# Round ends, table size and the place of the key matmul in a four-layer graph network kernel

## Chip, cores and metric

One core of one Trainium2 chip runs the whole program. The metric is the device time of one execution in microseconds (us). Engines: PE (TensorE, matmuls; PEld is its weight load), DVE (VectorE), ACT (ScalarE), POOL (GpSimd), SP (SyncE, which here only issues DMAs).

## What is computed

A graph of 3125 nodes with 32 features and 100,000 edges (src, dst, weight, 3 and 32 attributes) goes through four layers, each behind a layer norm and a ReLU and each added to x:

```
h = max(layernorm(x), 0);  x = x + L0(h)   # agg = segment_sum(edge_attr_32, src); dense 64 -> 128, batch norm, -> 32
h = max(layernorm(x), 0);  x = x + L1(h)   # radial net per edge and spherical harmonics, messages summed by dst
h = max(layernorm(x), 0);  x = x + L2(h)   # 3 times: out = clip(0.9 * A_w out + 0.1 h, 0, 1), A_w normalized weights
h = max(layernorm(x), 0);  x = x + L3(h)   # 3 times: z = batchnorm(relu(A_c z)), A_c normalized edge counts + self loop
```

A_w and A_c are 3125 by 3125 matrices, given only as edges.

## The kernel before

Nodes lie in 25 blocks of 128 (`NA`; 3200 with padding, `NP`), edges in 784 chunks of 128 (`CH`), worked through in 196 steps of four chunks (`STEPS`). The program has these stages.

**Zeroing** (0 to 213 us). POOL fills a DRAM table `both` with zeros by 40 DMAs: one pair (count, weight) of 8 bytes for each pair of nodes, 3200 by 3200 pairs.

**Phase 0** (some 50 to 1005 us), layer 0's sum over edges, while the edges are also put into the table. Four steps, k4 = 0 to 3, make one pass of a hardware loop. In each step PE multiplies a one-hot matrix with edge attributes (`scatter0`, L907, ten matmuls for two chunks, called a pair below). Beside it equal (src, dst) keys are found, so that POOL adds each key's sum once. A group is four chunks, two groups belong to a pass. `spread_keys` (L865, the **key matmul**) spreads a group's keys over the partitions into PSUM bank 7, the only one for it; ACT squares the differences (`compare_group`, L635, six operations) and makes 0/1 marks (L640); DVE keeps the earlier ones (`mark_group`, L1242); PE sums counts and weights per key (`merge_open`, L878 to L886, then `merge_hop` 1 to 3, L892, each of which waits for a flag of DVE, `live_entries`, L1290); DVE reads the result (`group_entries`, L1250 to L1255). One-hots come from ACT (L660, L665) and from DVE (L1304), the products that are multiplied from DVE (L1313). The row split of the attributes (L1301, L1309) belongs to k4 = 0. POOL's scatter-adds (L577) run beside all this, 782 in all, half of them before the feature table of layer 1 is there. Each engine runs its own list of instructions in order. On PE a step reads:

```
scatter0(s, k4, 0); scatter0(s, k4, 1)
if k4 % 2 == 0: merge_hop(g, slot, 2)
elif not is_last(s): merge_open(g, slot)
if k4 % 2 and not is_last(s, 4): spread_keys(g + 1, 1 - slot)
scatter0(s, k4, 2); scatter0(s, k4, 3)
if k4 % 2 == 0: merge_hop(g, slot, 3)
elif not is_last(s): merge_hop(g, slot, 1)
```

**Phase 1** (1060 to 2823 us), layer 1, with PE busy almost throughout.

**Rounds 0 to 2** (2825 to 3312 us), layer 2. In round 0 SP loads the table in 50 halves of a block of 128 rows (`big`, four slots); ACT takes out the weights and stores most to `adj_w` (nine blocks stay in SBUF, `kept`), DVE takes the row maxima of the counts and stores them as fp16 in `adj_c` through ACT's queue; PE multiplies (L1122). In rounds 1 and 2 the 16 streamed blocks of `adj_w` come back, and `group` (L1016) multiplies three blocks at once, on three of four column groups of 32; block 24 is a group by itself at the end. Each round ends with the sums copied out of PSUM by DVE and ACT (`copy_sums`, L1501 on DVE) and turned (L1108).

**Rounds 3 to 5** (3334 to 3481 us), layer 3 on the counts: PE multiplies three bf16 parts of z (`split_z`, in three portions of 5, 10 and 10 blocks) with the counts (L1063), first for 13 source blocks over all five banks, then the rest bank by bank; DVE reduces each bank (L1581 to L1584), takes mean and variance over the nodes (L1573 and a PE sum, L1098), and normalizes (L1597, L1598). Last, x is added (L1601), and SP stores the result.

The whole of what the change touches is printed here.

Of the kernel before, what the change touches and what calls it, by code (L numbers as in the profile page):

```python
# [25 lines left out]
P = 128  # L26
# [39 lines left out]
PER_ROUND = 2 * GROUPS + 1  # L66
# [3 lines left out]
BIG = NP * NP  # L70
CAP = 2048
SLOTS = 64
EIGHTH = NP // 8
# [4 lines left out]
EARLY = 13  # L78

# [7 lines left out]
def gnn_program(nc, x_in, src_in, dst_in, srcT_in, dstT_in, ea3_in, ea32_in, ew_in, ewT_in,  # L87
                w1T_in, b1_in, gamma_in, beta_in, w2T_in, b2_in, l1w1_in, l1b1_in, l1w2_in, l1b2_in,
                gam3_in, bet3_in, out):
    with ExitStack() as ctx:  # L90
# [296 lines left out]
        def load_half(eng, r, k, half, one):  # L387

            j = 4 * k + 2 * half + one
            m = STREAMED[2 * k + one]  # L390
            eng.dma_start(slots[:, j % 8, :],
                          adj_w[m * P:(m + 1) * P, half * HALF:(half + 1) * HALF]).then_inc(s_blk[j % 8], 16)
# [5 lines left out]
        def _(sp):  # L398
# [91 lines left out]

            pairs_of = both[0:BIG, :].rearrange("(s d) o -> s (d o)", d=NP)
# [16 lines left out]
            for r in range(1, 3):  # L508
# [19 lines left out]
            sp.wait_ge(s_out, 32)  # L528
# [3 lines left out]
        def _(pool):  # L532
# [70 lines left out]
            eighths = both[0:BIG, :].rearrange("(s d) o -> s (d o)", d=EIGHTH)  # L603
# [10 lines left out]
        def _(act):  # L614
# [125 lines left out]
            for j in range(2 * NA):  # L740
# [18 lines left out]
                if i < RING:  # L759
                    act.wait_ge(s_wcp, j + 1)  # L760
                    act.dma_start(adj_w[m * P:(m + 1) * P, half * HALF:(half + 1) * HALF],
                                  w_to).then_inc(s_wout[t], 16)
# [13 lines left out]
            def copy_sums(r):  # L776
                if r == 0:
                    act.wait_ge(s_half, NA)
                    act.wait_ge(s_full, NA)
                else:  # L780
                    act.wait_ge(s_mm, PER_ROUND * r)
# [23 lines left out]
            for r in range(1, 3):  # L805
                act.wait_ge(s_z, r + 1)

                def copy_z(g):
                    if g >= 2:
                        act.wait_ge(s_mm, PER_ROUND * (r - 1) + 2 * ((4 * g - 5) // 3 + 1))  # L810
                    n = min(4, NA - 4 * g)
# [25 lines left out]
        def _(pe):  # L837
# [86 lines left out]
            def phase0(s, k4, u):  # L924
# [7 lines left out]
                if k4 % 2 and not is_last(s, 4):  # L932
                    spread_keys(g + 1, 1 - slot)
# [66 lines left out]
            def spmm_round(r):  # L1000
                pe.wait_ge(s_z, r + 1)

                def group(k, blocks):

                    pe.wait_ge(s_zr, r * 7 + (blocks[-1] // 4 + 1))
                    for half in range(2):
                        values = []
                        for i in blocks[:-1]:
# [3 lines left out]
                        values.append(kept[:, k, half * HALF:(half + 1) * HALF])  # L1012
# [6 lines left out]
                        if k < GROUPS or half:  # L1019
                            mm.then_inc(s_mm, 1)  # L1020
# [115 lines left out]
        def _(dve):  # L1136
# [68 lines left out]
            V.scalar_tensor_tensor(out=keyT, in0=srcT, scalar=float(NP), in1=dstT, op0=ALU.mult, op1=ALU.add)  # L1205
            link(V.scalar_tensor_tensor(out=keyT_i, in0=srcT, scalar=float(NP), in1=dstT, op0=ALU.mult, op1=ALU.add))
# [5 lines left out]
            link(V.scalar_tensor_tensor(out=key[:, :], in0=src_i[:, :], scalar=float(NP), in1=dst_i[:, :],  # L1212
# [281 lines left out]
            def copy_sums(r):  # L1494
                if r == 0:
                    dve.wait_ge(s_half, NA)
                    dve.wait_ge(s_full, NA)
                else:
                    dve.wait_ge(s_mm, PER_ROUND * r)
                for n in (0, 2, 4):  # L1500
                    V.tensor_copy(aggT[:, n * 512:(n + 1) * 512], ps[:, n, :]).then_inc(s_aggc, 1)  # L1501
                dve.wait_ge(s_turn, r + 1)


            V.tensor_tensor(zn[:, :, :], h[:, :, :], over_f(dinv[:, 0, :]), ALU.mult).then_inc(s_z, 1)
# [11 lines left out]
            for r in range(3):  # L1517
                if r == 1:
                    link(V.tensor_tensor(slot_no[:, :], row_max[:, :, 0], row_max[:, :, 1], ALU.max))
                    V.tensor_scalar(flag[:, :], slot_no[:, :], float(CAP), None, ALU.is_gt).then_inc(s_flag, 1)  # L1520
# [17 lines left out]
            def split_z():  # L1538

                for a0, a1 in SPLITS:  # L1540
                    z, rest, to = zn[:, a0:a1, :], zrest[:, 0:a1 - a0, :], zparts[:, a0:a1, :, :]
# [19 lines left out]
            for e in range(8):  # L1561
# [5 lines left out]
                link(V.tensor_scalar(whole[SLOTS:P, :], whole[SLOTS:P, :], 9, None, ALU.arith_shift_right))  # L1567
                V.tensor_copy(over16[:, e * EIGHTH:(e + 1) * EIGHTH], whole).then_inc(s_over, 1)


            def over_nodes(i, r, src):

                V.tensor_reduce(fsum[:, 0, :], src.rearrange("p a f -> p f a"), AX, ALU.add).then_inc(s_fs, 1)  # L1573
# [3 lines left out]
            for r in range(3, 6):  # L1577
# [9 lines left out]
                link(V.tensor_scalar(fsum[:, 1, :], over_nodes(0, r, h[:, :, :]), 1.0 / NODES, None, ALU.mult))  # L1587
# [4 lines left out]
                V.tensor_scalar(fsum[:, 2, :], over_nodes(1, r, sq[:, :, :]), 1.0 / NODES, EPS,  # L1592
# [4 lines left out]
                link(V.tensor_tensor(sq[:, :, :], cen[:, :, :], over_a(fsum[:, 4, :]), ALU.mult))  # L1597
# [52 lines left out]
```

## Time and profile before

| what | us |
|---|---|
| median of three runs | 3483.51 |
| lowest and highest run | 3475.79, 3485.16 |
| the profiled execution, its own time | 3486.41 |
| its span in the trace | 3484.7 |

| busy in the span | us | share |
|---|---|---|
| PE | 2978.0 | 85% |
| DVE | 2742.2 | 79% |
| ACT | 2291.3 | 66% |
| POOL | 2104.3 | 60% |

The profile is one execution, taken by the hardware profiler. A timeline row gives an instruction's start, its length, engine, line, output and input; in brackets stands the idle time of the engine before it and what ended it. "issue" is time in which the engine waited for nothing that the profile shows. PEclk in a table of windows is the TensorE clock that was granted, 1.00 being 2.4 GHz. Busy shares over the whole span mix stages with different limits, so the windows of a stage say more.

### The profile page before, as it was taken

To read this page: it belongs to the slowest core of one execution; us is meant where nothing else is said; L and a number is where in the kernel's file an instruction comes from. 1 tells how busy PE (TensorE), PEld (TensorE's weight loads), DVE (VectorE), ACT (ScalarE), POOL (GpSimd) and SP (SyncE) were. 2 spreads that over 40 slices of the span, in tenths; PEclk is the share of its full clock that TensorE was granted. 3 is DMA by queue.
4 is the path that set the end of the run, shared out by engine and by line. 5 is a ranking of instruction groups with operands and counts; after the bars stand their busy time and mean duration, and the time that the engine had idled before them with its cause. 6 is when DMAs were issued, how large, how long until landed. Compare 5 with 4: busy or idle time off the path is not lost. (4 is left out here: it accounts for less than half of the span.)

```text
span 3484.7 us, 69264 instructions
## 1 busy us (share of the span) xinstructions
PE 2978.0 (85%) x19702; PEld 2385.9 (68%) x19703; DVE 2742.2 (79%) x5981; ACT 2291.3 (66%) x3192; POOL 2104.3 (60%) x1629
## 2 busy tenths in 40 slices
PE   3788788888877999999999999999999976657656
PEld 3677677777766888888888888888888841114256
DVE  6678888888877999999999999999999973450064
ACT  3678587877847888888888888888888832230000
POOL 4037888888866777777777777777777720000000
PEclk9999799899988999999999999999999987798878
DMA  9953222222213333333333333333333369999830
GB/s 402 422 188 36 12 15 16 14 15 15 15 6 67 52 50 52 52 52 50 52 52 51 52 52 52 50 52 52 51 51 52 52 242 426 425 389 377 362 139 6
DMA packets 265841, 397.89 MB, mean 114 GB/s; under 512 B 149901, under 2 KB 200836, under 8 KB 259252
## 3 DMA queue, kind: packets, MB, share of 16 engines
q0 software_dynamic: 149184, 124.54, 21.1%
q1 hardware_dynamic: 100180, 199.71, 16.9%
q10 hardware_dynamic: 16416, 72.92, 5.1%
q8 instruction: 28, 0.46, 0.1%
q14 instruction: 33, 0.27, 0.0%
HBM read 264.96 MB, written 132.05 MB: 114 GB/s over the span
## 5 line engine op out<-in xcount | busy, mean ns | idle before, releaser
L577 POOL DMA_INDIRECT both<-kept x782 | 1295.9, 1657 | 443.4 <-issue 205.1
L916 PEld LDWEIGHTS ps<-prod,big 128*128 128x128 f32 x7840 | 1134.3, 190 | 136.8 <-DVE prod L1283 133.2
L916 PE MATMUL ps<-prod,big 128*128 128x170 f32 x7840 | 1183.2, 310 | 22.2 <-DVE prod L1283 16.7
L585 POOL DMA_INDIRECT kept<-feat_dram,kept x782 | 760.8, 973 | 279.8 <-issue 232.2
L907 PE MATMUL ps<-prod,onehot 128*128 128x320 f32 x3920 | 719.4, 339 | 133.5 <-ACT onehot L665 116.2
L660 ACT ACTIVATE big<-iota_b,kept 128x640 f32<-128x640 f32 x1029 | 779.0, 815 | 13.6
L907 PEld LDWEIGHTS ps<-prod,onehot 128*128 128x128 f32 x3920 | 639.6, 207 | 167.9 <-issue 121.1
L665 ACT ACTIVATE big<-big 128x2560 f32<-128x2560 f32 x196 | 458.1, 2337 | 275.3 <-PE ps L916 275.2
L981 PE MATMUL ps<-w2mix,kept 65*128 65x384 f32 x1568 | 559.3, 500 | 21.6 <-ACT kept L712 21.6
L1455 DVE TENSOR_REDUCE kept<-kept 128x80 f32<-128x1280 f32 x392 | 562.0, 1474 | 0.0
L981 PEld LDWEIGHTS ps<-w2mix,kept 65*128 65x128 f32 x1568 | 284.1, 191 | 179.7 <-issue 23.5
L1445 DVE TENSOR_TENSOR kept<-ps,kept 128x384 f32<-128x384 f32 x784 | 396.3, 546 | 0.0
L608 POOL DMA_INDIRECT prod<-both,row_idx x8 | 7.8, 978 | 539.8 <-DVE row_idx L1560 525.8
L635 ACT ACTIVATE kept<-ps,kept 128x128 f32<-128x128 f32 (+2 forms) x588 | 225.0, 482 | 151.2 <-PE ps L865 151.2
L1313 DVE TENSOR_TENSOR prod<-kept 128x1280 fp32r<-128x1280 f32 x196 | 292.3, 1491 | 1.9
L1122 PE MATMUL ps<-big,zring 128*32 128x512 f32 (+3 forms) x400 | 184.8, 619 | 121.6 <-DMA big<-both 110.2
L1304 DVE TENSOR_SCALAR onehot<-iota_b,kept 128x640 fp32r<-128x640 f32 x539 | 285.7, 583 | 0.1
L1441 DVE TENSOR_TENSOR kept<-ps,kept 128x512 f32<-128x512 f32 x392 | 266.9, 681 | 0.0
L1122 PEld LDWEIGHTS ps<-big,zring 128*32 128x32 f32 x400 | 45.4, 125 | 261.0 <-issue 249.2
L1513 DVE TENSOR_REDUCE row_max<-big 128x1 f32<-128x1600 f32 x50 | 91.0, 1819 | 163.7 <-DMA adj_c<-kept 110.4
L757 ACT ACTIVATE kept<-big 128x1600 f32<-128x1600 f32 x50 | 82.2, 1648 | 192.3 <-issue 76.3
L1283 DVE TENSOR_TENSOR prod<-high,kept 128x680 f32<-128x680 f32 (+1 forms) x196 | 170.3, 869 | 43.8 <-DVE kept L1464 43.4
(232 smaller groups left out, 2988.8 us busy)
## 6 DMA issues: line engine op xcount, KB each, us to landing
both<-big POOLq DMA_DIRECT2D x40, 2000.0 KB, 96.2
big<-both SPq DMA_DIRECT2D x50, 1600.0 KB, 10.7
adj_w<-kept ACTq DMA_DIRECT2D x32, 800.0 KB, 33.3
big<-adj_w SPq DMA_DIRECT2D x32, 800.0 KB, 12.1
big<-adj_w ACTq DMA_DIRECT2D x32, 800.0 KB, 11.7
kept<-keys_dram SPq DMA_DIRECT2D x196, 128.0 KB, 3.0
kept<-in_wT SPq DMA_DIRECT2D x196, 128.0 KB, 3.0
adj_c<-kept ACTq DMA_DIRECT2D x42, 400.0 KB, 32.5
```

What stands on the lines that cost most here:

```text
L577: pool.indirect_dma_start(both, bass.IndirectOffsetOnAxis(ap=sc_idx[:, c:c + 1], axis=0), sc_val[:, c // 2, c % 2, :], None, compute_op=AL ...
L585: pool.indirect_dma_start(gath[:, s % 2, k, :], None, feat_dram, bass.IndirectOffsetOnAxis(ap=src_i[:, 4 * s + k:4 * s + k + 1], axis=0)). ...
L660: act.activation(dist[:, k, :], iota_b[:, :], ACT.Square, scale=-1.0, bias=bcol[:, ds(4 * s + k, 1)]).then_inc(s_dist[n], 4 // len(ks))
L665: act.activation(to[:, q, 0:len(ks), :], dist[:, 0:len(ks), :], ACT.Relu, scale=-1.0, bias=1.0).then_inc(s_oh[n], 1)
L907: mm = pe.matmul(ps[:, SUM0[part], 0:HI * 2 * FEAT], onehot0[:, q, k, part * P:(part + 1) * P], prod0[:, q, k, :, :].rearrange("p a m -> p ...
L916: mm = pe.matmul(part_sums(part, MSG), onehot[:, q, k, part * P:(part + 1) * P], prod[:, q, k, 0:HI * MSG], start=False, stop=False, skip_ ...
L981: mm = pe.matmul(ps[:, 4 + k, 0:384], hidT[:, q, k * P:(k + 1) * P], w2mix[:, :], start=True, stop=True)
L1304: ins = V.tensor_scalar(onehot0[:, q, k, :], iota_b[:, :], b_src[:, ds(4 * s + k, 1)], None, ALU.is_equal)
L1313: V.tensor_tensor(prod0[:, q, :, :, :], high0[:, ds(4 * s, 4), :].unsqueeze(3) .broadcast_to([P, 4, HI, 2 * FEAT]), rows0[:, 4 * k4:4 * k4 ...
L1441: V.tensor_tensor(T[:, :, 0:256].rearrange("p k (o x) -> p k o x", o=16), ps[:, 4 + 2 * g:6 + 2 * g, 0:256].rearrange("p k (o x) -> p k o ...
L1445: ins = V.tensor_tensor(T[:, k, 256:640].rearrange("p (u i x) -> p u i x", u=8, i=3), ps[:, 4 + 2 * g + k, 256:384].rearrange("p (u x) -> ...
L1455: V.tensor_reduce(res[:, q, 2 * g:2 * g + 2, 0:40], terms[:, g, :, :].rearrange("p k (o x) -> p k o x", x=16), AX, ALU.add).then_inc(s_red, 1)
```

## The change

1. *Key matmul.* `spread_keys` for the group after next is called in the even steps, behind `merge_hop` 2, instead of in the odd steps behind `merge_open`.
2. *Table.* `both` has 3126 rows (nodes and one for padding edges) of 3128 pairs. Zeroing, keys, loads and stores of round 0, loads of rounds 1 and 2 and the rows read for round 3 follow: second halves are 1528 columns wide instead of 1600, and block 24 is loaded with 54 rows.
3. *Last block in the last group.* Block 24 joins the eighth group, which now has four blocks.
4. *Sums copied by halves.* The banks that the first half of the last group completes are copied as soon as that half is done.
5. *Mean by bank.* In rounds 3 to 5 DVE sums each bank over its nodes when the bank is reduced.
6. *Normalization and result in portions.* The last two operations of a round go portion by portion, ahead of `split_z` for that portion; the result is normalized, added and stored in two portions.

The core of the diff, in which DVE's new function is called where the whole-width operations stood:

```diff
-PER_ROUND = 2 * GROUPS + 1
+PER_ROUND = 2 * GROUPS
-BIG = NP * NP
+TROWS = NODES + 1
+TCOLS = -(-TROWS // 8) * 8
+TABLE = TROWS * TCOLS
+BIG = -(-TABLE // (ZERO_PIECES * 2 * P)) * (ZERO_PIECES * 2 * P)
+WIDE = (HALF, TCOLS - HALF)
-EIGHTH = NP // 8
+EIGHTH = TCOLS // 8
+OUTS = ((0, 13), (13, NA))
...
-                sp.dma_start(big[:, j % 4, :],
-                             pairs_of[m * P:(m + 1) * P, half * NP:(half + 1) * NP]).then_inc(s_ld[j % 4], 16)
+                rows = min(P, TROWS - m * P)
+                sp.dma_start(big[0:rows, j % 4, 0:2 * WIDE[half]],
+                             pairs_of[m * P:m * P + rows, half * NP:half * NP + 2 * WIDE[half]]).then_inc(s_ld[j % 4], 16)
...
-            sp.wait_ge(s_fin, 1)
-            sp.dma_start(out[0:(NA - 1) * P, :].rearrange("(a b) f -> b a f", b=P),
-                         x[:, 0:NA - 1, :]).then_inc(s_out, 16)
+            for i, (a0, a1) in enumerate(OUTS):
+                sp.wait_ge(s_fin, i + 1)
+                whole = min(a1, NA - 1)
+                sp.dma_start(out[a0 * P:whole * P, :].rearrange("(a b) f -> b a f", b=P),
+                             x[:, a0:whole, :]).then_inc(s_out, 16)
...
                 for n in (1, 3, 5, 6):
                     c0, w = NCOL[n]
+                    if r == 0:
+                        act.wait_ge(s_half if n == 1 else s_full, NA)
+                    else:
+                        act.wait_ge(s_mm, PER_ROUND * r - (n == 1))
                     act.activation(aggT[:, c0:c0 + w], ps[:, n, 0:w], ACT.Copy).then_inc(s_agga, 1)
...
-                if k4 % 2 and not is_last(s, 4):
-                    spread_keys(g + 1, 1 - slot)
+                if k4 % 2 == 0 and not is_last(s, 4):
+                    spread_keys(g + 2, slot)
...
-                for k in range(GROUPS):
+                for k in range(GROUPS - 1):
                     group(k, (3 * k, 3 * k + 1, 3 * k + 2))
-                group(GROUPS, (NA - 1,))
+                group(GROUPS - 1, (NA - 4, NA - 3, NA - 2, NA - 1))
...
                 for n in (0, 2, 4):
+                    if r == 0:
+                        dve.wait_ge(s_full if n == 4 else s_half, NA)
+                    else:
+                        dve.wait_ge(s_mm, PER_ROUND * r - (n < 4))
                     V.tensor_copy(aggT[:, n * 512:(n + 1) * 512], ps[:, n, :]).then_inc(s_aggc, 1)
...
+            def normal(r, a0, a1):
+
+                n = a1 - a0
+                link(V.tensor_tensor(h[:, a0:a1, :], cen[:, a0:a1, :],
+                                     fsum[:, 4, :].unsqueeze(1).broadcast_to([P, n, FEAT]), ALU.mult))
+                link(V.tensor_tensor(h[:, a0:a1, :], h[:, a0:a1, :],
+                                     bet3[:, r - 3, :].unsqueeze(1).broadcast_to([P, n, FEAT]), ALU.add))
...
+                    link(V.tensor_reduce(fsum[:, 5 if b else 0, :], h[:, mine, :].rearrange("p a f -> p f a"), AX,
+                                         ALU.add))
+                    if b:
+                        ins = V.tensor_tensor(fsum[:, 0, :], fsum[:, 0, :], fsum[:, 5, :], ALU.add)
...
-                link(V.tensor_tensor(sq[:, :, :], cen[:, :, :], over_a(fsum[:, 4, :]), ALU.mult))
-                link(V.tensor_tensor(h[:, :, :], sq[:, :, :], over_a(bet3[:, r - 3, :]), ALU.add))
                 if r < 5:
-                    split_z()
-            V.tensor_tensor(x[:, :, :], x[:, :, :], h[:, :, :], ALU.add).then_inc(s_fin, 1)
+                    split_z(r)
+            for a0, a1 in OUTS:
+                normal(5, a0, a1)
+                V.tensor_tensor(x[:, a0:a1, :], x[:, a0:a1, :], h[:, a0:a1, :], ALU.add).then_inc(s_fin, 1)
```

How the order of instructions changes at three places. (ISA and REGISTER_ALU rows are waits and address arithmetic; lines of the change are numbered in its own file: L872 is the key matmul, L899 a hop, L914 the pair, L1024 `group`, L1115 the turn.)

PE, phase 0, in the loop before, an odd step from the end of `merge_open` to the first pair of the next even step and its hop 2:

```order
L886 MATMUL ps<-kept 128x1
L862 ISA
L864 REGISTER_ALU
L865 MATMUL ps<-kept,places 128x512
L907 MATMUL ps<-prod_49,onehot_50 128x320 x10
L892 MATMUL ps<-kept 128x1
L902 REGISTER_ALU
L905 ISA
L907 MATMUL ps<-prod_49,onehot_50 128x320 x10
L892 MATMUL ps<-kept 128x1
```

And in the changed kernel, an even step from its first pair to hop 3:

```order
L914 MATMUL ps<-prod_49,onehot_50 128x320 x10
L898 ISA
L899 MATMUL ps<-kept 128x1
L869 ISA
L871 REGISTER_ALU
L872 MATMUL ps<-kept,places 128x512
L914 MATMUL ps<-prod_49,onehot_50 128x320 x10
L898 REGISTER_ALU
L899 MATMUL ps<-kept 128x1
```

The key matmul stood behind the last matmul of `merge_open` (L886), ahead of the odd step's second pair; it now stands between hop 2 and hop 3, ahead of the even step's second pair.

PE, end of round 1 before, the second half of the eighth group (`big` holds two streamed blocks, `kept` the third), then block 24 alone, then the turn:

```order
L1016 MATMUL ps<-big,zring 32x512 x2
L1016 MATMUL ps<-kept,zring 32x512
L1016 MATMUL ps<-big,zring 32x128 x2
L1016 MATMUL ps<-kept,zring 32x128
L1016 MATMUL ps<-kept,zring 32x512 x3
L1016 MATMUL ps<-kept,zring 32x64
L1016 MATMUL ps<-kept,zring 32x448
L1016 MATMUL ps<-kept,zring 32x512 x2
L1016 MATMUL ps<-kept,zring 32x128
L1108 MATMUL ps<-stack_id,prod 128x32 x25
```

And in the changed kernel:

```order
L1024 MATMUL ps<-big,zring 32x512 x2
L1024 MATMUL ps<-kept,zring 32x512 x2
L1024 MATMUL ps<-big,zring 32x128 x2
L1024 MATMUL ps<-kept,zring 32x128 x2
L1115 MATMUL ps<-stack_id,prod 128x32 x25
```

The eight matmuls of the lone block are gone from behind the group; each piece of the group has two of `kept` instead of one.

DVE, end of round 5 before, from the variance on:

```order
L1592 TENSOR_SCALAR fsum<-ps 128x32
L1595 RECIPROCAL fsum<-fsum 128x32
L1596 TENSOR_TENSOR fsum<-fsum,gam 128x32
L1597 TENSOR_TENSOR both_tmp<-both_tmp,fsum 128x800
L1598 TENSOR_TENSOR h<-both_tmp,bet 128x800
L1601 TENSOR_TENSOR x<-x,h 128x800
```

And in the changed kernel:

```order
L1620 TENSOR_SCALAR fsum<-ps 128x32
L1623 RECIPROCAL fsum<-fsum 128x32
L1624 TENSOR_TENSOR fsum<-fsum,gam 128x32
L1586 TENSOR_TENSOR h<-both_tmp,fsum 128x416
L1588 TENSOR_TENSOR h<-h,bet 128x416
L1629 TENSOR_TENSOR x<-x,h 128x416
L1586 TENSOR_TENSOR h<-both_tmp,fsum 128x384
L1588 TENSOR_TENSOR h<-h,bet 128x384
L1629 TENSOR_TENSOR x<-x,h 128x384
```

The three operations of full width became two portions of three, and the first portion's result is there before the second is begun.

## Rows read from the trace of the kernel before

**Rows 1.** Windows: length, busy PE, PEld, DVE, ACT, POOL, PEclk, DMA share, GB/s.
```profile
100.00:200.00 100.00, 78.95 (x562) 69.44 (x561) 70.86 (x161) 70.57 (x111) 0.00 (x0) 0.95 1.02 422
220.00:1005.00 785.00, 661.39 (x4652) 590.43 (x4651) 649.60 (x1371) 605.46 (x934) 646.21 (x385) 0.90 0.26 17
2900.00:3050.00 150.00, 93.29 (x182) 22.34 (x183) 59.74 (x45) 35.27 (x24) 0.00 (x0) 0.76 1.01 426
```

**Rows 2.** Waits, 600 to 1000 us: waiting line, releaser, us in total, times, longest.
```profile
ACT kept L635 <- PE ps L865: 56.2, 42, 2.3
PE ps L907 <- ACT onehot L665: 54.1, 33, 2.1
```

**Rows 3.** Timeline of ACT, phase 0, first comparison of a set of four steps.
```profile
681.45 2.30 ACT L635 ACTIVATE kept<-ps,kept 128x128 f32<-128x128 f32 x6 [0.97 <-PE ps L865]
...
701.45 2.30 ACT L635 ACTIVATE kept<-ps,kept 128x128 f32<-128x128 f32 x6 [2.30 <-PE ps L865]
...
718.95 2.30 ACT L635 ACTIVATE kept<-ps,kept 128x128 f32<-128x128 f32 x6 [0.98 <-PE ps L865]
...
981.33 2.29 ACT L635 ACTIVATE kept<-ps,kept 128x128 f32<-128x128 f32 x6 [2.31 <-PE ps L865]
```

**Rows 4.** Windows, the stretch behind 690 us, columns as in rows 1.
```profile
690.00:695.00 5.00, 5.00 (x30) 4.35 (x29) 3.07 (x6) 3.67 (x7) 4.39 (x3) 0.50 0.33 28
```

**Rows 5.** Timeline of PE, phase 0.
```profile
688.20 1.85 PE L907 MATMUL ps<-prod,onehot 128*128 128x320 f32 x10 [2.09 <-ACT onehot L665]
...
708.20 1.73 PE L907 MATMUL ps<-prod,onehot 128*128 128x320 f32 x10 [2.07 <-ACT onehot L665]
...
710.18 0.38 PE L865 MATMUL ps<-kept,places 3*128 3x512 bf16 x1
710.50 1.73 PE L907 MATMUL ps<-prod,onehot 128*128 128x320 f32 x10
...
712.11 1.73 PE L907 MATMUL ps<-prod,onehot 128*128 128x320 f32 x10
```

**Rows 6.** Timeline of DVE, phase 0.
```profile
706.18 0.16 DVE L1290 TENSOR_SCALAR kept<-ps 128x1 bf16<-128x1 f32 x1
...
710.42 1.49 DVE L1313 TENSOR_TENSOR prod<-kept 128x1280 fp32r<-128x1280 f32 x1
...
715.50 0.16 DVE L1290 TENSOR_SCALAR kept<-ps 128x1 bf16<-128x1 f32 x1
...
718.60 1.49 DVE L1313 TENSOR_TENSOR prod<-kept 128x1280 fp32r<-128x1280 f32 x1
```

**Rows 7.** Timeline of POOL, the first add and the first load of the feature table.
```profile
222.06 1.90 POOL L577 DMA_INDIRECT both<-kept  x1 [181.14 <-DMA both<-big]
...
1058.52 1.02 POOL L585 DMA_INDIRECT kept<-feat_dram,kept  x1 [35.10 <-DMA feat_dram<-big]
```

**Rows 8.** Timeline of DVE, end of round 0.
```profile
3137.32 1.89 DVE L1501 COPY prod<-ps 128x512 f32<-128x512 f32 x3 [3.15 <-issue]
```

**Rows 9.** Chain of waits, end of round 1: start, us, what.
```profile
3196.70 12.61 DMA big<-adj_w
...
3209.44 2.89 PE ps L1016 x26
...
3212.41 4.26 PE ps L1016 x13
...
3216.69 0.70 DVE prod L1501
```

**Rows 10.** Chain of waits, end of round 4 and start of round 5.
```profile
3424.25 0.34 DVE h L1583
...
3424.97 1.50 DVE fsum L1573
...
3433.86 1.00 DVE h L1598
...
3436.99 15.75 PE ps L1063 x325
```

More of the change, by code:

```diff
@@ L390, in load_half @@
             m = STREAMED[2 * k + one]
-            eng.dma_start(slots[:, j % 8, :],
-                          adj_w[m * P:(m + 1) * P, half * HALF:(half + 1) * HALF]).then_inc(s_blk[j % 8], 16)
+            eng.dma_start(slots[:, j % 8, 0:WIDE[half]],
+                          adj_w[m * P:(m + 1) * P, half * HALF:half * HALF + WIDE[half]]).then_inc(s_blk[j % 8], 16)
         block = ctx.enter_context(nc.Block())
@@ L760, in _ @@
                     act.wait_ge(s_wcp, j + 1)
-                    act.dma_start(adj_w[m * P:(m + 1) * P, half * HALF:(half + 1) * HALF],
-                                  w_to).then_inc(s_wout[t], 16)
+                    act.dma_start(adj_w[m * P:(m + 1) * P, half * HALF:half * HALF + WIDE[half]],
+                                  w_to[:, 0:WIDE[half]]).then_inc(s_wout[t], 16)
                 act.wait_ge(s_ccp, j + 1)
@@ L1007, in group @@
                         values = []
-                        for i in blocks[:-1]:
+                        for i in blocks[:2]:
                             j = 4 * k + 2 * half + len(values)
@@ L1011, in group @@
                             values.append(slots[:, j % 8, :])
-                        values.append(kept[:, k, half * HALF:(half + 1) * HALF])
+                        for i in blocks[len(values):]:
+                            values.append(kept[:, k + i - blocks[2], half * HALF:(half + 1) * HALF])
                         for c0, w, bank, col in pieces[half]:
@@ L1204, in _ @@
             dve.wait_ge(s_in["idxT"], 32)
-            V.scalar_tensor_tensor(out=keyT, in0=srcT, scalar=float(NP), in1=dstT, op0=ALU.mult, op1=ALU.add)
-            link(V.scalar_tensor_tensor(out=keyT_i, in0=srcT, scalar=float(NP), in1=dstT, op0=ALU.mult, op1=ALU.add))
+            V.scalar_tensor_tensor(out=keyT, in0=srcT, scalar=float(TCOLS), in1=dstT, op0=ALU.mult, op1=ALU.add)
+            link(V.scalar_tensor_tensor(out=keyT_i, in0=srcT, scalar=float(TCOLS), in1=dstT, op0=ALU.mult, op1=ALU.add))
             V.tensor_scalar(digit_i[:, 0, :], keyT_i, 16, None, ALU.arith_shift_right)
@@ L1211, in _ @@
             dve.wait_ge(s_in["idx"], 32)
-            link(V.scalar_tensor_tensor(out=key[:, :], in0=src_i[:, :], scalar=float(NP), in1=dst_i[:, :],
+            link(V.scalar_tensor_tensor(out=key[:, :], in0=src_i[:, :], scalar=float(TCOLS), in1=dst_i[:, :],
                                         op0=ALU.mult, op1=ALU.add))
@@ L1519, in _ @@
                     link(V.tensor_tensor(slot_no[:, :], row_max[:, :, 0], row_max[:, :, 1], ALU.max))
-                    V.tensor_scalar(flag[:, :], slot_no[:, :], float(CAP), None, ALU.is_gt).then_inc(s_flag, 1)
+                    V.scalar_tensor_tensor(out=flag[:, :], in0=slot_no[:, :], scalar=float(CAP), in1=valid[:, :],
+                                           op0=ALU.is_gt, op1=ALU.mult).then_inc(s_flag, 1)
                 copy_sums(r)
@@ L1536, in _, with split_z @@
             layernorm()
-            def split_z():
+            def split_z(r=None):
                 for a0, a1 in SPLITS:
+                    if r is not None:
+                        normal(r, a0, a1)
                     z, rest, to = zn[:, a0:a1, :], zrest[:, 0:a1 - a0, :], zparts[:, a0:a1, :, :]
@@ L1591, in _ @@
                 link(V.tensor_tensor(sq[:, :, :], cen[:, :, :], cen[:, :, :], ALU.mult))
[L1592 removed]
+                V.tensor_reduce(fsum[:, 0, :], sq[:, :, :].rearrange("p a f -> p f a"), AX, ALU.add).then_inc(s_fs, 1)
+                V.tensor_scalar(fsum[:, 2, :], over_nodes(1, r), 1.0 / NODES, EPS,
                                 ALU.mult, ALU.add).then_inc(s_var, 1)
@@ L1625, in chunks @@
         return a.reshape((CH, P) + a.shape[1:]).swapaxes(0, 1).reshape(P, -1)
-    src, dst = (chunks(k, NP - 1) for k in ("src", "dst"))
+    src, dst = (chunks(k, NODES) for k in ("src", "dst"))
     w = chunks("edge_weight", 0)
```

35 lines of the change are left out of this document (15 added, 20 removed).

## The prediction, made before the change was timed

> **What bounds the kernel now.** I read the windows first, to split the 3484.7 us into stretches with different limits, then waits and timelines inside those that the change touches. The profiled execution took 3486.4 us, 2.9 above the median of the three runs (3483.5), so I sum against 3486.4 and take 2.9 off at the end. A difference of 0.3% (10.5 us) is about what a measurement of this kernel can tell from none. Zeroing the table and round 0 run at the rate of the DMA engines, 422 and 426 GB/s at a share of 1.0 [rows 1]; there bytes are time. Phase 0 (220 to 1005 us) is held by no single engine: no busy time fills its 785 us [rows 1], so a loop of waits sets it. Phase 1 is not touched.
>
> In phase 0 the reader should see one loop. ACT's group comparison waits for the key matmul, 42 times and 56 us in 400; PE waits for ACT's one-hots, 33 times and 54 us [rows 2]. From 701.45 to 718.95 four steps take 17.50 us; from 681.45 to 701.45 they take 20.00; from 701.45 to 981.33, 15 sets of four, the mean is 18.66 [rows 3]. In the 20.00 PE's clock is at 1.2 instead of 2.4 GHz for a stretch, 0.50 granted with PE full [rows 4]. Just before, PE had stood still for 2.09 us waiting for ACT (688.20). An equal pause, 2.07 us at 708.20 [rows 5], lies in the 17.50 set. So the plain loop is 17.50, a fall of the clock costs about 2.5, and (18.66 - 17.50) / 2.5 = 0.46 falls come per set. 785 / 18.66 gives 42 sets; I count 41, leaving one out for work that the stretch holds once.
>
> **The key matmul.** It moves from the odd step, behind merge_open, into the even step before, behind hop 2. Same count; what changes is what stands ahead of it. ACT's path (key matmul 710.18 [rows 5], compare, one-hots, pair on PE, merge_open, key matmul) opens: the keys are there one to two pairs earlier. Left is the loop between DVE and PE. On DVE hop 3 is seen at 715.50, then come group entries, marks and one-hots up to the product at 718.60, 3.10 us, and the product, 1.49 [rows 6]. On PE, pair and hop take 712.11 - 710.50 = 1.61 and the key matmul 710.50 - 710.18 = 0.32 [rows 5], so two pairs with hops and the key matmul, which this loop now carries, are 3.54. That is 8.1 us for a half; the half with the row split starts at 706.18 and reaches its product at 710.42: 4.24 + 1.49 + 3.54 = 9.3. Their sum is 17.4, plus four handovers between engines of some 0.1: 17.8. I take 17.7; the bounds are 17.4, with no handover, and 18.1, with handovers of nearly 0.2. The loop itself thus gains nothing: +0.2 a set. Nor should the matmul wait for its row bank, since ACT's first six squares (2.30 us from their start [rows 3]) come before that point.
>
> What moves is PE's pause. The single wait of two microseconds for ACT goes; waits for the product of some 1.3 remain. If half the falls go, a set loses 0.58 instead of 1.16: 17.7 + 0.58 = 18.28, -0.38 by 41 = **-15**. Bounds: all falls gone, -40, and POOL, which waits 35.1 us for the feature table [rows 7], allows some 44 with its earlier start; one fall in every set, 17.7 + 2.5 = 20.2, **+63**. I take the middle because half of the long pauses here were followed by no fall. The loads of key parts on SP's queue are released by the key matmul of two groups before, so they move with it and keep a lead of a whole set, and the attribute loads queued behind them come no later: nothing. If that lead were short, the next key matmul would be late, which is case D.
>
> **The table.** 3126 rows of 3128 pairs instead of 3200 by 3200: 78.2 MB instead of 81.9, 3.7 MB at 422 GB/s = 8.8 us less zeroing. It lets POOL start at 213 instead of 222.06, and this is hidden behind POOL's 35.1 us [rows 7]. Phase 0 beside it wins the little that it runs faster without the DMA load, **-1** (0 to -2). In round 0 each of 24 second halves loads 576 bytes a row less (1.77 MB), the last block 54 rows instead of 128 (1.92 MB), and the stores of weights are narrower (0.59 MB): 4.28 MB / 426 = 10.0 us. The end of that stretch isn't bound by bytes: the copies start at 3137.32, after 3.15 in which DVE waits for a last store, past all loads [rows 8]; that tail stays. I take **-8** between -10 and -3. The low end is for stores that end little earlier than now, and for the row pitch of 25,024 bytes, which is no multiple of 256: the nearest rows with different streams, 422 and 426, differ by 1%, 2 us on the 78 MB read here.
>
> The Trainium skill has two rules against this part, which no run here shows yet. "DMA: Bandwidth & Descriptors", how a descriptor splits into AXI transactions: one that starts off a 256-byte boundary fetches from the boundary below. Estimated from that page, some 3 beats on 400 a row, 1.4 us for the whole read. The same page, why a DMA increments its semaphore by 16: the engines used are the largest number up to 16 that divides the rows, so 54 rows would go by 9; the last 1.35 MB would take 5.6 us instead of 3.2, and my -8 would be about -4.
>
> **The ends of rounds 1 and 2.** The lone last block costs 4.26 us on the chain behind the last three-block half of 2.89 [rows 9]. Now it rides as a fourth column group with the other three, on rows of the array that they leave free. If a half with four costs what one with three does, all 4.26 goes; if it adds by matmuls, 2.89 by 4/3 is 0.96 more and -3.3 is left. Copying the first half's sums while the second runs hides the 0.70 of DVE at 3216.69 [rows 9]. Narrower loads, 0.59 MB a round, give 1 where DMA bounds the round (12.61 us of load in the chain). I take **-6** for round 1 and **-5** for round 2, whose end is bound by PE; bounds -13 and -7 together. In round 0 the split copies gain nothing, since that last store precedes them.
>
> **The count rounds.** A mean by bank: rounds 4 and 5 have DVE waiting between banks, so only the last bank's reduce (0.34, as the operation of that width at 3424.25) and a small add, some 0.2 by estimate, stand in place of 1.50 [rows 10]: -0.9 each. In round 3, where DVE runs the banks back to back, five reduces and four adds replace it: +1.0. The normalization in portions: the first fifth needs two operations of 0.34 instead of two of 1.00 [rows 10], -1.3 in rounds 3 and 4. PE's early pass takes 15.75 us for 13 source blocks [rows 10], so 6 for the first five; the second portion's eight operations of some 0.5 lie under it, uncovered they would cost 1. Result in two portions: two more small operations, half the output earlier, -0.2. Together +1.0 - 1.8 - 2.6 - 0.2 = -3.6, **-4** (-5 to 0).
>
> **Sum.** -15 - 1 - 8 - 6 - 5 - 4 = -39; 3486.4 - 39 = 3447.4, less 2.9: 3444.5, **3445**.
>
> **The rivals.**
> (A) *The clock stays up.* With the long pause gone, no falls: -40 instead of -15, 3420. For it: such a pause stands ahead of the fall at 690. Against it: the pause at 708.20 did nothing.
> (B) *Falls in every set, the slower case.* The pauses before the products recur in each half, evenly, and the clock falls once a set: +63 in place of -15, 3445 + 78 = 3523. It decides from a loss of (39 - 15) / 41 = 0.59 us a set over today's: then the other gains are used up, 3484. For it: today's sets already show 0.46 falls without anything that prevents more. Against it: PE's pauses become shorter.
> (C) *Falls as before, and a loop as long as I take it or longer.* 17.7 to 18.1 plus 1.16: +0.2 to +0.6 by 41 = +8 to +25, the rest -24: 3468 to 3485. For it: DVE is busy 650 of 785 us [rows 1], and the key matmul now stands in its loop; PE does the same work in sets of about the old length. The Trainium skill ("TensorE: Matmul & The Clock Gate", part 1) has the clock set "based on how busy the PE has been recently"; by that rule moved pauses alone change nothing, and this case holds. The trace so far bears it out in one thing, that an equal pause is followed by a fall only at times.
> (D) *The move doesn't open ACT's loop*, since the matmul must wait for ACT's squares from the group before (one row bank): phase 0 as now, 3460.
>
> **How the numbers follow.** My forecast 0.40, A 0.23, B 0.08, C 0.22, D 0.07. Faster by more than 0.3% (under 3473): forecast, A, D and 0.08 of C, 0.78. Within: 0.13 of C. Slower: B and the last of C, 0.09. The range from 3413 (A with the best of the other bounds) to 3484 (C) leaves B and some margin out.
>
> **What would show it.** ACT's wait for the key matmul nearly gone and PE's for ACT's one-hots with it, PE's weight loads waiting for DVE's product instead; compares every 17.4 to 18.1 us where the clock holds; granted clock over phase 0 above 0.90 (A: near 1; B: 0.83 or less). POOL's first add near 213 and its wait for the feature table longer than 35, or shorter if phase 0 shrinks by more. Round 0's last copy 8 us earlier relative to its start, the lone group of 4.26 absent. I am wrong if phase 0 lasts as long as before with a steady clock, if the load of 54 rows is slow, or if the four-block half takes 7 us.

## The result, and the profile after

The changed kernel takes 3462.99 us (median of 7 runs, 3448.94 to 3469.85) against 3482.31 for the kernel before: a ratio of 0.994, 95% interval 0.9929 to 0.9952. It is faster, by 19 us; 38 were forecast. (Each ratio here is to the kernel before, timed beside the kernel in question.) The profiled execution has a span of 3465.3 us, 19.4 below that of before, so the stages can be compared directly. Each line of the table runs from one event in the two traces to the next:

| stage, from one event to the next | before | after | difference | forecast |
|---|---|---|---|---|
| start to POOL's first gather from the feature table | 1058.5 | 1057.6 | -0.9 | -16 |
| to DVE's first reduction of round 0 | 1776.4 | 1774.9 | -1.5 | 0 |
| to the copies of round 0's sums | 302.4 | 298.8 | -3.6 | -8 |
| to the end of round 1's turn | 86.6 | 81.6 | -5.0 | -6 |
| to the end of round 2's turn | 98.3 | 92.8 | -5.5 | -5 |
| to the end (rounds 3 to 5, result) | 162.5 | 159.7 | -2.8 | -4 |

The events in the changed kernel are POOL's first gather (1057.58) and DVE's first reduction (2832.51) in the rows below, the copies at 3131.27, and the DVE operation behind each turn (the chain's rows L1531). Of before, the three that stand in no group of rows are these, from the timeline of DVE and from the chain of waits:

```profile
2834.95 1.82 DVE L1513 TENSOR_REDUCE row_max<-big 128x1 f32<-128x1600 f32 x1
```

```profile
3223.92 1.07 DVE both_tmp L1523 x2
...
3322.18 1.07 DVE both_tmp L1523 x2
```

Most of what is missing, 15 of 20 us, is missing ahead of phase 1. There the changed kernel's rows look as if the change had worked. Windows, as [rows 1]:

```profile
220.00:1005.00 785.00, 675.75 (x4749) 582.40 (x4749) 670.73 (x1421) 604.17 (x948) 654.38 (x365) 0.98 0.25 17
```

Waits from 600 to 950 us, as [rows 2]:

```profile
ACT onehot L673 <- PE ps L914: 48.9, 20, 2.7
PEld ps L914 <- DVE prod L1320: 35.5, 39, 1.5
PE ps L914 <- DVE prod L1320: 32.2, 39, 1.4
```

Timeline of ACT, first comparison of a set, as [rows 3]:

```profile
432.27 2.28 ACT L643 ACTIVATE kept<-ps,kept 128x128 f32<-128x128 f32 x6
...
699.78 2.28 ACT L643 ACTIVATE kept<-ps,kept 128x128 f32<-128x128 f32 x6
...
717.45 2.28 ACT L643 ACTIVATE kept<-ps,kept 128x128 f32<-128x128 f32 x6
...
931.54 2.28 ACT L643 ACTIVATE kept<-ps,kept 128x128 f32<-128x128 f32 x6
```

The granted clock is 0.98 where it was 0.90. ACT's wait for the key matmul has left the list, PE and its weight loads wait for DVE's product, and ACT waits for PE instead. A set of four steps takes 17.67 us (699.78 to 717.45), and 17.83 as the mean of 28 sets (432.27 to 931.54), where the mean was 18.66. So phase 0 did get shorter, by 28.6 us up to the point where SP stores the finished feature table (timeline of SP, before and changed):

```profile
1051.95 0.38 SPq L454 DMA_DIRECT2D feat_dram<-big  x1
```

```profile
1023.34 0.38 SPq L459 DMA_DIRECT2D feat_dram<-big  x1
```

But POOL's timeline, as [rows 7], takes it back:

```profile
211.90 1.68 POOL L585 DMA_INDIRECT both<-kept  x1 [170.98 <-DMA both<-big]
...
1055.73 1.54 POOL L585 DMA_INDIRECT both<-kept  x1 [0.30 <-issue]
1057.58 1.02 POOL L593 DMA_INDIRECT kept<-feat_dram,kept  x1 [0.30 <-issue]
```

The adds begin 10 us earlier and end 34 us later. The 35 us in which POOL waited for the feature table are gone, not because the table is late but because POOL is. 392 adds take 1057.3 - 211.9 = 845 us, 2.16 each; before it was (1023.4 - 222.1) / 392 = 2.04.

### The profile page after: what moved, and what is told of

Same layout as the page of the kernel before. It is cut to its first block and busy times, and to the rows that moved or that the text cites. A ratio compares the mean times of both kernels' runs of the same rounds, so it can differ in the third digit from the quotient of the medians.

```text
span 3465.3 us, 69301 instructions
## 1 busy us (share of the span) xinstructions
PE 2974.6 (86%) x19703; PEld 2370.4 (68%) x19703; DVE 2742.9 (79%) x6018; ACT 2280.7 (66%) x3192; POOL 2141.3 (62%) x1629
## 3 DMA queue, kind: packets, MB, share of 16 engines
q1 hardware_dynamic: 100034, 195.42, 16.6%
## 5 line engine op out<-in xcount | busy, mean ns | idle before, releaser
L585 POOL DMA_INDIRECT both<-kept x782 | 1333.0, 1705 | 439.8 <-issue 194.6
L923 PE MATMUL ps<-prod,big 128*128 128x170 f32 x7840 | 1183.2, 310 | 22.5 <-DVE prod L1290 17.4
L668 ACT ACTIVATE big<-iota_b,kept 128x640 f32<-128x640 f32 x1029 | 779.0, 815 | 13.6
L914 PE MATMUL ps<-prod,onehot 128*128 128x320 f32 x3920 | 684.5, 325 | 81.2 <-DVE prod L1320 79.6
L914 PEld LDWEIGHTS ps<-prod,onehot 128*128 128x128 f32 x3920 | 597.7, 194 | 112.9 <-DVE prod L1320 84.5
L1311 DVE TENSOR_SCALAR onehot<-iota_b,kept 128x640 fp32r<-128x640 f32 x539 | 291.4, 593 | 0.0
L673 ACT ACTIVATE onehot<-big 128x640 fp32r<-128x640 f32 x196 | 171.1, 873 | 182.4 <-PE ps L914 173.7
```

The source lines that it names most:

```text
L585: pool.indirect_dma_start(both, bass.IndirectOffsetOnAxis(ap=sc_idx[:, c:c + 1], axis=0), sc_val[:, c // 2, c % 2, :], None, compute_op=AL ...
L668: act.activation(dist[:, k, :], iota_b[:, :], ACT.Square, scale=-1.0, bias=bcol[:, ds(4 * s + k, 1)]).then_inc(s_dist[n], 4 // len(ks))
L673: act.activation(to[:, q, 0:len(ks), :], dist[:, 0:len(ks), :], ACT.Relu, scale=-1.0, bias=1.0).then_inc(s_oh[n], 1)
L914: mm = pe.matmul(ps[:, SUM0[part], 0:HI * 2 * FEAT], onehot0[:, q, k, part * P:(part + 1) * P], prod0[:, q, k, :, :].rearrange("p a m -> p ...
L923: mm = pe.matmul(part_sums(part, MSG), onehot[:, q, k, part * P:(part + 1) * P], prod[:, q, k, 0:HI * MSG], start=False, stop=False, skip_ ...
L1311: ins = V.tensor_scalar(onehot0[:, q, k, :], iota_b[:, :], b_src[:, ds(4 * s + k, 1)], None, ALU.is_equal)
```

## Experiments

The theory, P: POOL's adds are the path from the end of the zeroing to phase 1, and the moved matmul makes each of them slower. The rivals: the table's new row pitch slows them (Q), or the moved matmul brought its share and something else took it (R).

### The key matmul alone, and all but the key matmul

The first is the kernel before with

```diff
-                if k4 % 2 and not is_last(s, 4):
-                    spread_keys(g + 1, 1 - slot)
+                if k4 % 2 == 0 and not is_last(s, 4):
+                    spread_keys(g + 2, slot)
```

> The kernel before with the key matmul moved and nothing else. Theory P (POOL's scatter-adds took over as the bound): phase 0 on PE, DVE and ACT ends some 40 us earlier, with the granted clock near 0.98 over it, but the 392 adds start at 222 us as before and take 2.16 us each instead of 2.04, so they end at about 1068; POOL no longer waits for the feature table, and the kernel is about 9 us slower than before, 3491 us. Rival Q (the new table's row pitch slows the adds, not the moved matmul): adds at 2.04, ending at 1023, and the kernel is 35 us faster, 3447.

The second is the changed kernel with these lines as they were before.

> The changed kernel with the key matmul put back. P: the clock falls again, phase 0 ends near 1004, the adds take 2.04 us each and end near 1013, POOL waits some 40 us for the feature table, phase 1 starts near 1057 as in the changed kernel: the same time within 4 us, 3463. Rival Q: adds at 2.16 with the old place of the matmul too. Rival R (the moved matmul did bring its 15 us, and something else took them): 3478.

Measured: the matmul alone makes the kernel slower, 3496.31 us, ratio 1.0035 (1.0017 to 1.0053). Everything but the matmul gives 3464.36 us, ratio 0.9948 (0.9931 to 0.9966), the changed kernel's time. POOL's timeline with the matmul alone, then with all but it:

```profile
220.64 1.90 POOL L577 DMA_INDIRECT both<-kept  x1 [179.73 <-DVE kept L1255]
...
1064.35 1.02 POOL L585 DMA_INDIRECT kept<-feat_dram,kept  x1 [0.30 <-issue]
```

```profile
1055.41 1.02 POOL L593 DMA_INDIRECT kept<-feat_dram,kept  x1 [40.66 <-DMA feat_dram<-big]
```

The adds' groups from 430 to 940 us (count, busy time, mean ns), in this order: before, changed, matmul alone, all but the matmul:

```profile
L577 POOL DMA_INDIRECT both<-kept x253 | 421.8, 1667 | 88.3 <-issue 88.3
```

```profile
L585 POOL DMA_INDIRECT both<-kept x238 | 427.3, 1796 | 84.5 <-issue 78.6 <-DMA both<-kept 4.2 <-DVE kept L1262 1.7
```

```profile
L577 POOL DMA_INDIRECT both<-kept x238 | 428.8, 1802 | 82.0 <-issue 78.5 <-DMA both<-kept 3.5
```

```profile
L585 POOL DMA_INDIRECT both<-kept x254 | 420.3, 1655 | 90.2 <-issue 86.8 <-DMA both<-kept 3.4
```

An add takes 1.80 us wherever the matmul has moved and 1.66 wherever it hasn't, with either table. Q falls, R too. What the moved matmul gives on PE it costs on POOL, and with the new table it hardly matters whether POOL or the feature table is last: 1057.6 against 1055.4.

### Why an add becomes slower

Two adds from the changed kernel's timelines beside DVE's products:

```profile
608.13 1.49 DVE L1320 TENSOR_TENSOR prod<-kept 128x1280 fp32r<-128x1280 f32 x1
...
612.78 1.48 DVE L1320 TENSOR_TENSOR prod<-kept 128x1280 fp32r<-128x1280 f32 x1
```

```profile
608.38 2.65 POOL L585 DMA_INDIRECT both<-kept  x1 [0.30 <-issue]
611.34 1.54 POOL L585 DMA_INDIRECT both<-kept  x1 [0.30 <-issue]
613.34 2.33 POOL L585 DMA_INDIRECT both<-kept  x1 [0.46 <-issue]
```

Both long adds start inside a product and end 1.41 us behind its end (608.38 + 2.65 against 608.13 + 1.49; 613.34 + 2.33 against 612.78 + 1.48); the one between takes its plain 1.54. From 430 to 940 us, 48 of the 238 adds start inside a product and are lengthened by it, to 2.33 us each, and end 1.41 to 1.44 us behind the product's end. In the kernel before it is 37 of 253, 2.10 us each, with the same distance. Adds that start in the last 0.13 us of a product aren't lengthened, which fits: 1.54 - 0.13 = 1.41. The product holds the add up until it ends, and in the changed kernel more adds meet one, and nearer to its start.

The product isn't the only operation that does it. The row split's two operations do too, L1308 (one SBUF input) and L1316 (two), as these rows of DVE and of POOL show, with ends 1.41 and 1.42 us apart:

```profile
601.77 0.42 DVE L1308 TENSOR_SCALAR kept<-kept 128x512 int32<-128x512 int32 x1
...
603.81 0.67 DVE L1316 TENSOR_TENSOR kept<-kept 128x512 f32<-128x512 f32 x1
```

```profile
601.82 1.78 POOL L585 DMA_INDIRECT both<-kept  x1 [0.30 <-issue]
603.91 1.99 POOL L585 DMA_INDIRECT both<-kept  x1 [0.30 <-issue]
```

DVE's one-hots (L1311) do it as well. All the adds' time over 1.54 us from 430 to 940 us is 60.8 us in the changed kernel (0.26 an add) and 32.1 before (0.13). The products make 37.9 of it, the row split 15.0, the one-hots 7.7; before it was 20.6, 1.6 and 9.7. So the products are some 60% of what an add lost, and the row split, which hardly any add met before, is the rest.

The Trainium skill ("SBUF — State Buffer", SBUF: two separate sides) has VectorE and GpSimd share one pair of ports, as an exclusive lock: an operation of VectorE in a 2-port mode, or one with two SBUF inputs against a GpSimd operation that reads SBUF, takes it for the whole instruction if it starts first. The holds by the products and by L1316 agree with that; whether L1308 and L1311 run in a 2-port mode no run shows. By the same rule a GpSimd operation that starts first keeps the other out for its whole length, and in that the trace doesn't agree: 92 of the changed kernel's 114 products start while an add is under way for more than 0.06 us, and none of these takes more than 1.50 us.

If the product holds the adds, shorter products must hold them for less:

```diff
-                V.tensor_tensor(prod0[:, q, :, :, :], high0[:, ds(4 * s, 4), :].unsqueeze(3)
+                for o in (0, 2):
+                    V.tensor_tensor(prod0[:, q, o:o + 2, :, :], high0[:, ds(4 * s + o, 2), :].unsqueeze(3)
...
```

> The changed kernel with DVE's product of a step of phase 0 in two halves of 0.75 us. If an add that meets a product waits for that one instruction to end, the halves cut the delay: adds at some 2.05 us, POOL done near 1016, 3463 - 40 = 3423. If adds lose by DVE's total time, or by something else: adds at 2.16 as before, 3463, or a little more for the added DVE instructions.

Measured: 3446.96 us, ratio 0.9894 (0.9878 to 0.9911), 16 us under the changed kernel. The adds' group again, and the first gather:

```profile
L585 POOL DMA_INDIRECT both<-kept x250 | 423.9, 1696 | 89.0 <-issue 85.1 <-DVE kept L1262 2.3 <-DMA both<-kept 1.6
```

```profile
1039.96 1.02 POOL L593 DMA_INDIRECT kept<-feat_dram,kept  x1 [16.56 <-DMA feat_dram<-big]
```

The adds end at 1023.4, 2.07 us each, near the 2.05 that the theory had; from 430 to 940 us the products hold them for 16.8 us instead of 37.9, though DVE's work is longer. Only now the feature table is last, at 1040, so the gain is 16 and not 40. (The longer DVE work makes a set 18.0 us.)

### What POOL's queue is worth, and phase 1's pace

Leave 24 adds out, and nothing else: `for c in range(CH // 2 - 24): add(c)`, with the later counts of landed adds lowered by 12 for each parity.

> The changed kernel without the last 24 of the 392 adds that go ahead of layer 1 (chunks 368 to 391 never reach the table, so the time is that of 24 adds fewer). P: 24 x 2.16 = 52 us less on POOL, the feature table at about 1018 is then last, phase 1 starts there: 3463 - 39 = 3424. If phase 1's start isn't held by POOL's adds: 3463.

Measured: 3442.29 us, ratio 0.9884 (0.9867 to 0.9902): 21 us, where 39 were expected.

```profile
1028.08 1.02 POOL L595 DMA_INDIRECT kept<-feat_dram,kept  x1 [22.78 <-DMA feat_dram<-big]
```

Phase 1 starts 29.5 us earlier, behind the feature table, which I had put at 1018 and which lands at 1028. The profiled spans, of one execution each, differ by 26.9 us, the medians by 21. So 29.5 us is what the changed kernel loses to POOL's adds at the start of phase 1. Can the adds simply go later?

```diff
-            for c in range(CH // 2):
+            for c in range(CH // 2 - 24):
                 add(c)
...
+                    late = max(0, 24 - (s - BEHIND + 1) // 8)
+                    upto = min(2 * (STEPS + s - BEHIND) + 2 - late, USED)
+                    for c in range(added[0], upto):
+                        add(c)
```

> The changed kernel with 24 of the 392 adds ahead of layer 1 moved into phase 1, one more in every eighth step. Theory P2 (POOL also sets phase 1's pace, its queue never waits there by more than 0.3 us): phase 1 starts at 1028 as in drop24, but takes 24 x 1.9 = 46 us more: 3463 - 29 + 46 = 3480. Rival (PE sets phase 1's pace and POOL has slack): 3442 as in drop24.

> As shift24, but the 24 adds come in twos, one pair more in every sixteenth step, so that an even add never follows the odd one it waits for within a step more often than in the changed kernel; in shift24 the odd shift put such a wait of up to 3.5 us in half the steps. P2 (POOL sets phase 1's pace): start at 1028, phase 1 longer by 24 x 1.9 = 46 us: 3480. Rival (POOL has slack in phase 1): 3442 as in drop24.

Measured: 3735.93 us, ratio 1.0722 (1.0699 to 1.0745), and in pairs 3522.81 us, ratio 1.0111 (1.0093 to 1.0129). The first was a badly made experiment. In the second half of the edges an even add waits until the odd one before it has landed; the shift by one put the two side by side, as in this row of its timeline, in step after step:

```profile
1804.39 1.58 POOL L586 DMA_INDIRECT both<-kept  x1 [2.20 <-issue]
```

In pairs this is left to about a dozen steps. First gather and first reduction of round 0 there:

```profile
1033.70 1.02 POOL L594 DMA_INDIRECT kept<-feat_dram,kept  x1 [24.57 <-DMA feat_dram<-big]
```

```profile
2890.89 1.82 DVE L1525 TENSOR_REDUCE row_max<-big 128x1 f32<-128x1600 f32 x1
```

That is 1857 us instead of 1775: 82 more, 46 of them for 24 adds of 1.9 us, most of the rest in thirteen such waits of 2.1 to 3.1 us, 34 in all. There is no slack to shift into; POOL sets phase 1's pace too. PE's busy share there, 98% (1731.6 of the 1763 us from 1060 to 2823 in the changed kernel), hid it: POOL's own waits from 1100 to 2800 are of 0.3 us at most.

### The table alone

The changed kernel with `TROWS = NP` (and the two operations that clear the columns beyond the table left out, since there are none):

> The changed kernel with the table at 3200 by 3200 pairs again. Theory P (POOL is the bound from the end of the zeroing to the end of phase 1): POOL starts its adds 9 to 10 us later and all of it arrives, phase 1 starts at 1067; with round 0 longer by 4 and the other rounds by 1 or 2, 3463 + 15 = 3478 us. By the recorded prediction the zeroing is hidden and round 0 is worth 8: 3463 + 10 = 3473, with phase 1 starting at 1058.

Measured: 3485.91 us, ratio 1.0011 (0.9995 to 1.0026).

```profile
220.48 1.68 POOL L585 DMA_INDIRECT both<-kept  x1 [179.57 <-DMA both<-big]
...
1071.17 1.02 POOL L593 DMA_INDIRECT kept<-feat_dram,kept  x1 [0.30 <-issue]
```

Without the smaller table nothing is left of the gain: phase 1 starts 12.7 us later than in the kernel before, and the 13.4 us that the last four parts of the change give in rounds 1 to 5 only make up for it. Against the changed kernel, POOL starts 8.6 us later and gathers 13.6 later (its adds take 2.17 instead of 2.16); round 0 takes 303.7 instead of 298.8. The table is worth 18.6 us in the profiled spans and 23 in the medians, of which I had booked 9, and the zeroing's part of it at nothing.

### The last block's load

> The changed kernel with each load of block 24 (54 rows) cut into 48 and 6 rows. Theory (a load of 54 rows goes by few DMA engines: the last loads ran at 111 to 209 GB/s where the kernel before had 418 to 438): the last loads come back to over 300 GB/s and the time from DVE's first reduction of round 0 to its copies of the sums falls from 298.8 us by 2 to 5. Rival (the end waits for stores of counts): 298.8 as it is.

The edit: `for r0, r1 in ((0, 48), (48, 54))`, two loads for each half of block 24. One execution, 3466.17 us. Timeline of DVE, first reduction, the first wait of the tail, the copies; first of the changed kernel, then with the loads cut:

```profile
2832.51 1.82 DVE L1520 TENSOR_REDUCE row_max<-big 128x1 f32<-128x1600 f32 x1
...
3103.60 1.82 DVE L1520 TENSOR_REDUCE row_max<-big 128x1 f32<-128x1600 f32 x1 [9.40 <-DMA adj_c<-prod]
...
3115.73 1.82 DVE L1520 TENSOR_REDUCE row_max<-big 128x1 f32<-128x1600 f32 x1 [4.70 <-DMA adj_c<-prod]
...
3131.27 1.89 DVE L1507 COPY prod<-ps 128x512 f32<-128x512 f32 x3 [3.17 <-issue]
```

```profile
2832.20 1.82 DVE L1522 TENSOR_REDUCE row_max<-big 128x1 f32<-128x1600 f32 x1
...
3104.12 1.82 DVE L1522 TENSOR_REDUCE row_max<-big 128x1 f32<-128x1600 f32 x1 [9.69 <-DMA adj_c<-prod]
...
3131.48 1.89 DVE L1509 COPY prod<-ps 128x512 f32<-128x512 f32 x3 [3.15 <-issue]
```

299.3 us against 298.8: nothing. Nor did the last loads' rate come back (238, 151 and 133 GB/s in the 5 us from 3110, 3115 and 3120). The tail waits for stores of counts to free their staging, 9.4, 2.0, 4.7 and 1.7 us ahead of four of its last six reductions, and 9.7, 2.0, 4.4, 1.0 and 0.7 with the loads cut. So the rule of the Trainium skill ("DMA: Bandwidth & Descriptors", why a DMA increments its semaphore by 16) by which 54 rows go by 9 engines is neither shown nor refuted here; the 2.4 us estimated from it don't show in the stage's time.

### Looking for a faster kernel

Three more cuts of the product, each with PE waiting for less than the whole: in the first `scatter0` waits for `4 * s + (2 if k < 2 else 4)` of the halves' increments, in the second only in odd steps, in the third there are four quarters and it waits for `4 * s + k + 1`.

> As split_prod, and PE's first two scatters of a step wait for the first half of the product alone. In split_prod POOL's adds ended at 1023 and the feature table at 1040 was last (3447 us), so there PE, DVE and ACT's loop was the bound again. Theory: the loop between DVE and PE loses most of one half-product, 0.7 us, per pair of steps, the feature table is ready before 1020, and POOL is last again at 1025 to 1045, since denser products slow its adds: 3432 to 3450 us. Rival: the loop is not that of DVE and PE, and the first half buys nothing: 3447.

Measured: 3453.58 us, ratio 0.9907 (0.9885 to 0.9929). A set falls to 16.6 us (29 sets from 429.2 to 911.1), so it was the loop between DVE and PE that set a set's length. The last copy into the feature table starts at 974.1, but POOL arrives at 1045.0, 2.12 us an add: more than 60 us of slack for PE, DVE and ACT, and a slower kernel than with plain halves.

```profile
974.10 0.42 DVE L1427 COPY big<-h 128x400 f32<-128x400 f32 x1
```

```profile
1045.00 1.03 POOL L593 DMA_INDIRECT kept<-feat_dram,kept  x1 [0.30 <-issue]
```

> As split_prod, with PE's first two scatters waiting for the first half of the product in the odd steps alone. In split_prod the feature table was last, 17 us behind POOL's adds, in split_prod2 POOL was last, at 2.12 us an add. Theory P: in between, adds at 2.09 end near 1032, the feature table near 1030: 3438 to 3445. Rival (the adds' rate hangs on how POOL and DVE happen to fall into step, not on density alone): anything from 3440 to 3460, not between its neighbours 3447 and 3454.

Measured: 3451.59 us, ratio 0.9905 (0.9888 to 0.9922). It lies between its neighbours, not below them: the adds end at 1020.1 (2.06 us each), but a set takes 18.0 us and the feature table comes last, at 1044.6. That waiting for half a product in odd steps alone would shorten the loop was wrong.

> The changed kernel with a step's product in four quarters of some 0.4 us, and each chunk's scatter on PE waiting for its own quarter. In split_prod2 a set of four steps took 16.6 us and the feature table was issued at 974.5, but POOL's adds, at 2.12 us each, ended at 1045. Theory P (an add that starts inside a product waits for that instruction's end): shorter holds, adds at 2.00 to 2.05 us, done at 997 to 1016; the feature table is there before 1000; phase 1 starts at 1000 to 1016 and the time is 3405 to 3422 us. Rival (quarters back to back hold POOL as one product does): adds at 2.12 and more, 3453 or slower.

Measured: 3445.13 us, ratio 0.9876 (0.986 to 0.9893). It has the lowest median of the kernels that compute everything, though 2 us under split_prod are within the spread of the runs. The adds came to 2.09 us, not 2.00 to 2.05, and end last, with the feature table long there:

```profile
1034.06 1.02 POOL L593 DMA_INDIRECT kept<-feat_dram,kept  x1 [0.31 <-issue]
```

Most adds that a quarter holds (65 of 76 from 430 to 940 us) do end 1.41 us behind that quarter; 11 wait for a later one. What the quarters save on the products, 20.8 us of holds instead of 37.9, is partly lost again to the one-hots, 17.3 instead of 7.7: in the denser loop more adds start in those. What makes an add start in one operation rather than in another stays open.

## Why the prediction was right and where it failed

The sign and the range held; the forecast gain was twice the measured one. That the range held is in part luck: its end at 3484 was made for a falling clock (case C), and no term in it allowed for slower adds. The time is also near case D's 3460, whose mechanism did not happen: ACT's loop did open. By its steps:

**The loop.** Right: 17.7 us for a set, bounds 17.4 and 18.1, measured 17.83 in the mean, with PE waiting for the product as foretold; split_prod2, where PE waits for half of it, has 16.6.

**The clock.** I took half the falls; nearly all went (0.98). That is case A. The moved matmul does it (0.97 with it alone, 0.90 with all but it, from 220 to 1005 us); that it does so by taking away the long pause, as case A has it, isn't shown by itself. Case B fell. Case C, that moved pauses alone change nothing, fell too: sets a little longer than the old plain ones, the same work, and hardly a fall. The sentence of the Trainium skill quoted there ("TensorE: Matmul & The Clock Gate", part 1) isn't refuted by that, only what I made of it; which of PE's pauses matters isn't settled here.

**POOL's cover.** This is the step that failed: "POOL, which waits 35.1 us for the feature table, allows some 44 with its earlier start". It took the 392 adds at their old 2.04 us. With DVE's products and row split more in the way they take 2.16, 392 x 0.11 = 44 us, and the whole allowance is gone. So -15 became -0.9 together with the table's part, though the feature table was 28.6 us earlier. The trace of before already had the price: 37 adds held by a product took 2.10 us instead of 1.54.

**The zeroing.** "Hidden behind POOL's 35.1 us": it was the visible part. Once POOL is last, each microsecond of an earlier start arrives, and table_old shows it does. With the matmul in its old place the zeroing would have been hidden as I had it, since the feature table is last there (1055.4), and the kernel is just as fast. So of the two parts the moved matmul brings nothing beside the new table, and a loss of 12 us without it.

**Round 0.** -3.6 for -8. "That tail stays" was right, but I took only 2 us off for it. From 3110 us on the DMA engines moved 209, 178 and 111 GB/s in stretches of 5 us, so bytes weren't time for the last 20 us. (The "about -4" that the prediction gives for a slow last load doesn't follow from its own numbers: 5.6 - 3.2 = 2.4 us more is -5.6. The -3.6 is no sign of that rule.)

**Rounds 1 and 2.** -5.0 and -5.5 for -6 and -5. A four-block half costs what a three-block one does, 2.93 against 2.89 [rows 9], and the copy of the half hides except for ACT's last piece:

```profile
3202.24 2.93 PE ps L1024 x32
...
3205.59 0.61 ACT prod L791
...
3206.24 6.57 PE ps L1115 x42
...
3212.83 1.06 DVE both_tmp L1531 x2
...
3305.58 1.07 DVE both_tmp L1531 x2
```

**The count rounds.** Round 4 gave -2.25 (start to start of PE's early pass) for -2.2. In the chain, as [rows 10], a bank's reduce is 0.43 and its add 0.20 in place of 1.50, and the first portion's two operations 0.34 each:

```profile
3408.44 0.43 DVE fsum L1606
...
3408.89 0.20 DVE fsum L1609
...
3415.45 0.34 DVE h L1586
...
3418.28 16.74 PE ps L1070 x325
```

Round 3 lost 0.15 instead of gaining 0.3, and round 5's early pass took 16.74 instead of 15.75 [rows 10], at a granted clock of 0.82 for 0.88, which I had not counted.

## What to carry to other kernels

An engine that waits at a stage's end has slack only at its present rate: before you spend that slack, look at what slows its single instructions and whether your change makes more of it. Run the parts of a change one at a time in both directions, alone on the old kernel and left out of the new one, since what hides a part is often another part. And an engine that is busy 98% may still follow another one, whose waits are all too short to be noticed.

## What was not expected of the hardware

An indirect DMA instruction of POOL that starts while DVE multiplies two SBUF operands, more than 0.05 us behind the product's start and more than 0.13 us before its end, ends 1.41 to 1.44 us behind that end, in every kernel looked at (before, changed, all but the matmul, product in halves). An operation of DVE with one SBUF input (L1308) holds it in the same way: 20 adds, with the same distance, in the changed kernel. The other way round, products that started more than 0.06 us into such an instruction weren't held (92 of 114, none over 1.50 us). Cutting a 1.49 us product into halves, 1.56 us together, cost DVE 0.07 us and took 0.09 us off the mean of 392 adds.
